# One kernel of six sublayers: two tensors for the scatter-adds of the first expert layer, and smaller edits at the ends of three stages

## Chip, core and metric

The kernel runs on one core of one Trainium2 chip. The metric is device time in microseconds from launch to end. Engines are named as in the profile: PE is TensorE, DVE VectorE, ACT ScalarE, POOL GpSimd, SP SyncE (here it only issues DMAs). One profiled execution gives every number of the trace.

## What is computed

Tokens are 8192 rows of 128 numbers. Six sublayers follow each other, each on the layer-normed (attention and routed feed-forward) or plain stream:

```python
x = x + 0.5 * _L0_ffn_ref(_layernorm(x), ...)    # f1: light local attention on all tokens, heavy attention on routed ones
x = x + _L0_attn_ref(_layernorm(x), ...)         # la: causal attention with latent q, k, v
x = x + 0.5 * _L0_ffn_ref(_layernorm(x), ...)    # f2
x = x + 0.5 * _L1_ffn_ref(_layernorm(x), ...)    # m1: top-6 of 64 experts, and a shared expert
x = x + _L1_attn_ref(_layernorm(x), ...)         # ca: attention with normalized q and k, no mask
x = x + 0.5 * _L1_ffn_ref(_layernorm(x), ...)    # m2: as m1
```

What matters of the expert layer and of the attention after it:

```python
def _L1_ffn_ref(x, ...):          # 64 experts, 6 of them per token
...
    hmid = gelu(einsum('ech,ehf->ecf', xs, w1))
    y = einsum('ecf,efh->ech', hmid, w2).reshape(E * CAP, h)
    y_pair = y[slot] * pair_w[:, None]
    out = zeros((t, h)).at[token_of].add(y_pair)
    shared = gelu(x @ sw1.T) @ sw2.T
    return out + shared
...
def _L1_attn_ref(x, ...):
    qkv = x @ in_proj_weight.T + in_proj_bias
    attn = softmax(l2_normalize(q) @ l2_normalize(k).T * ls)
```

In `_L0_attn_ref` q, k and v are `(x @ W_down) @ W_up`, half of each head's q and k turned by rope: pairs (x1, x2) become (-x2, x1) times a sine and added. In `_L0_ffn_ref` a routing score is the dot product of each normed token with two routing tokens.

## The kernel before

The stream stays on chip in `g_x` or `g_y` (128 partitions x 64 tiles of 128 numbers); `routed_ffn` (f1, f2), `stacked_attention` (la, ca) and `moe_block` (m1, m2) run one after another, and each begins when all engines have finished the one before. Within a stage every engine has its own instruction list, written out by hand as a function `body`, and the engines wait for each other by semaphores only.

**Expert layer, `moe_block`.** The base of the result (`m_ob`: stream and shared expert) is stored to the DRAM tensor `x_after_experts`. The picked tokens are worked on in 24 chunks of 128 rows, three to a group. POOL gathers a chunk (`gather`, line 2218: an indirect DMA from `gather_table` into `m_xs`); PE transposes it (line 2332) and multiplies by the experts' weights (2342, 2353, 2363, the last sums rows of equal token within a chunk); ACT copies a group's three results into `m_yc` (2422), one of two buffers. POOL then adds each chunk to `x_after_experts` by an indirect DMA with an add (line 2252). A token's rows can stand in several chunks, so a scatter-add waits until the one before it has landed (`scattered`), and only then goes out; after it POOL issues the gather of the chunk six further on. m2 does the same into `out_x`.

**Dense attention, `stacked_attention(latent=False)`.** It reads the stream back from `x_after_experts`: ACT's queue loads `g_y` in four parts of 16 tiles (1 MB each), SP's queue the weights, the biases, `ca_ones`, and rows of a block pattern. The attention is pipelined over 16 batches of 4 tiles; bodies -3, -2 and -1 fill the pipeline. `part_stats` (1872 to 1887) makes the layer norm's scale `g_a` and shift `g_b` of one part on DVE: 16 statistics (1876) and six small operations, with ACT's `deviation` (1751, 1753) in between. Part 0 comes ahead of body -3, parts 1, 2 and 3 at the ends of bodies -3, -2 and -1. In each body ACT makes the normed tiles `ca_xn` (1849), PE transposes them (1717), ACT copies them to `ca_xnT` (1858), PE multiplies (1580, 1666), ACT and DVE normalize (1924, 1839, 1841), POOL splits q and k into three bf16 parts (`split`, 1335 to 1347), SP stores those to `stack_image` (1299) and loads them back as `ca_qs`, `ca_ks` (1308). From body -1 on PE makes the scores (1484) and DVE their maxima (1936), 16 per body.

**Latent attention, its tail.** In every batch POOL multiplies the new stream with the routing tokens (`route_dots`, 1398) and sums the products by halving in seven steps (1408); the last batch's stand at the end of the stage.

**First light attention, its tail.** Here the weights `fw_weff` of the latent attention are made: products of `W_down` and `W_up` for q, k, v and two turned copies, whose `W_up` DVE has turned and negated before (`f1l_up`, 693 to 702, in front of the maximum of line 651). PE makes them in 5 x 8 fp32 products, which the profile shows as 80 instructions (553); ACT copies them (620, 621).

## Time and profile before

| | us |
|---|---|
| median of three runs | 3169.9 (3168.26 to 3171.17) |
| the profiled execution | 3158.49 |
| its span, first to last instruction | 3156.8 |

Where the stages lie in the span: f1 0 to 800 (its light attention ends at 542), la 800 to 1533, f2 1533 to about 2270, m1 from there to 2492 (its scatters 2388.6 to about 2487), ca 2492.8 to about 2930, m2 to the end. PE is busy for 86% of the span, DVE 73%, ACT and POOL 58% and 50%. In the profile an engine's idle time stands in brackets behind the instruction it ended at, with what ended it. "issue" means that nothing visible was waited for. A name ending in q (SPq, POOLq) is the engine's queue. Buffer numbers are left out.

### The profile page before, as it was taken

To read this page: it belongs to the slowest core of one execution; us is meant where nothing else is said; L and a number is where in the kernel's file an instruction comes from. 1 tells how busy PE (TensorE), PEld (TensorE's weight loads), DVE (VectorE), ACT (ScalarE), POOL (GpSimd) and SP (SyncE) were. 2 spreads that over 40 slices of the span, in tenths; PEclk is the share of its full clock that TensorE was granted. 3 is DMA by queue.
4 is the path that set the end of the run, shared out by engine and by line. 5 is a ranking of instruction groups with operands and counts; after the bars stand their busy time and mean duration, and the time that the engine had idled before them with its cause. 6 is when DMAs were issued, how large, how long until landed. Compare 5 with 4: busy or idle time off the path is not lost. (4 is left out here: it accounts for less than half of the span.)

```text
span 3156.8 us, 72883 instructions
## 1 busy us (share of the span) xinstructions
PE 2729.0 (86%) x24406; PEld 1826.4 (58%) x24406; DVE 2288.7 (73%) x6052; ACT 1825.7 (58%) x3760; POOL 1591.3 (50%) x1872
## 2 busy tenths in 40 slices
PE   7999998999599999999788999899895369998874
PEld 4777887777233333333477888677773135555652
DVE  5998775888489988887488777699782267775741
ACT  3777664555156666666477666455551148786521
POOL 1222323876447766664322232577555356662555
PEclk9999998999689999999899999899995569998875
DMA  4000000000233333331000000000063346553532
GB/s 112 1 0 1 1 0 1 1 0 1 74 82 82 82 82 77 76 75 41 14 0 0 1 1 0 1 1 0 18 158 69 81 124 151 143 140 92 145 91 30
DMA packets 155616, 161.59 MB, mean 51 GB/s; under 512 B 42001, under 2 KB 133905, under 8 KB 154641
## 3 DMA queue, kind: packets, MB, share of 16 engines
q1 hardware_dynamic: 145616, 146.90, 18.7%
q0 software_dynamic: 9216, 7.87, 1.9%
q10 hardware_dynamic: 576, 4.19, 0.3%
q8 instruction: 113, 1.85, 0.3%
q14 instruction: 95, 0.77, 0.1%
HBM read 83.24 MB, written 74.60 MB: 50 GB/s over the span
## 5 line engine op out<-in xcount | busy, mean ns | idle before, releaser
L1938 DVE CUSTOM_DVE_ANT_0 la_ps<-la_ps,la_tri 128x512 f32<-128x512 f32 (+3 forms) x1024 | 481.5, 514 | 93.6 <-PE la_ps L1484 86.6
L1762 ACT ACTIVATE la_prob<-la_ps 128x512 f32<-128x512 f32 x640 | 373.8, 602 | 240.2 <-PE la_ps L1495 233.2
L475 POOL TENSOR_TENSOR f2l_prob<-f2l_prob,f2l_rec 128x512 f32<-128x512 f32 x128 | 133.0, 1060 | 330.6 <-DVE f2l_rec L673 330.6
L475 POOL TENSOR_TENSOR f1l_prob<-f1l_prob,f1l_rec 128x512 f32<-128x512 f32 x128 | 133.0, 1060 | 328.5 <-DVE f1l_rec L673 328.5
L1484 PE MATMUL la_ps<-la_ks,la_qs 48*128 48x512 bf16 (+3 forms) x1024 | 255.0, 317 | 47.2 <-DVE la_mx L1938 29.2
L1350 POOL TENSOR_SCALAR_AFFINE_SELECT la_prob<-la_prob 128x512 f32<-128x512 f32 x256 | 159.3, 634 | 208.9 <-ACT la_prob L1762 208.6
L1495 PE MATMUL la_ps<-la_qs,la_ks 50*128 50x512 bf16 (+3 forms) x1024 | 241.4, 308 | 5.2 <-ACT la_prob L1762 2.2
L1936 DVE TENSOR_REDUCE ca_mx<-ca_ps 128x4 f32<-128x512 f32 x256 | 173.7, 687 | 90.9 <-PE ca_ps L1484 89.6
L1495 PEld LDWEIGHTS la_ps<-la_qs,la_ks 50*128 50x128 bf16 x1024 | 66.9, 94 | 234.7 <-ACT la_prob L1762 163.1
L1762 ACT ACTIVATE ca_prob<-ca_ps 128x512 f32<-128x512 f32 x256 | 152.1, 602 | 85.0 <-PE ca_ps L1495 85.0
L1527 PE MATMUL la_ps_o<-la_prob,la_v 128*32 128x512 f32 (+3 forms) x2048 | 196.0, 456 | 0.0
L1938 DVE DVE_READ_ACCUMULATOR2_ANT la_mx<- 128x1 f32 x1024 | 144.8, 141 | 0.0
L1484 PEld LDWEIGHTS la_ps<-la_ks,la_qs 48*128 48x128 bf16 x1024 | 67.1, 95 | 115.9 <-DVE la_mx L1938 92.6
L504 PE MATMUL f2l_ps_qk<-f2l_xrT,fw_wqkv 128*128 128x128 f32 x1024 | 133.0, 284 | 0.7 <-ACT f2l_xrT L609 0.7
L504 PE MATMUL f1l_ps_qk<-f1l_xrT,fw_wqkv 128*128 128x128 f32 x1024 | 133.0, 284 | 0.7 <-ACT f1l_xrT L609 0.7
L504 PEld LDWEIGHTS f2l_ps_qk<-f2l_xrT,fw_wqkv 128*128 128x128 f32 x1024 | 120.7, 194 | 11.7 <-issue 10.5
L504 PEld LDWEIGHTS f1l_ps_qk<-f1l_xrT,fw_wqkv 128*128 128x128 f32 x1024 | 120.7, 194 | 11.7 <-issue 10.5
L592 ACT ACTIVATE f2l_prob<-f2l_ssub 128x1024 f32<-128x1024 f32 x64 | 67.8, 1059 | 85.4 <-DVE f2l_ssub L655 82.7
L592 ACT ACTIVATE f1l_prob<-f1l_ssub 128x1024 f32<-128x1024 f32 x64 | 67.7, 1058 | 80.5 <-DVE f1l_ssub L655 80.5
L1484 PE MATMUL ca_ps<-ca_ks,ca_qs 56*128 56x128 bf16 x1024 | 99.0, 225 | 5.2 <-DVE ca_mx L1936 3.0
L1495 PE MATMUL ca_ps<-ca_qs,ca_ks 58*128 58x128 bf16 x1024 | 99.4, 224 | 4.4 <-ACT ca_prob L1762 3.4
L1495 PEld LDWEIGHTS ca_ps<-ca_qs,ca_ks 58*128 58x128 bf16 x1024 | 58.4, 96 | 71.0 <-ACT ca_prob L1762 36.8
(539 smaller groups left out, 7977.8 us busy)
## 6 DMA issues: line engine op xcount, KB each, us to landing
stack_image<-la_parts SPq DMA_DIRECT2D x192, 128.0 KB, 2.4
stack_image<-ca_parts SPq DMA_DIRECT2D x192, 128.0 KB, 2.4
la_qs<-stack_image SPq DMA_DIRECT2D x64, 192.0 KB, 3.6
la_ks<-stack_image SPq DMA_DIRECT2D x64, 192.0 KB, 4.4
ca_qs<-stack_image SPq DMA_DIRECT2D x64, 192.0 KB, 3.5
ca_ks<-stack_image SPq DMA_DIRECT2D x64, 192.0 KB, 4.5
gather_table<-fw_wqkv SPq DMA_DIRECT2D x16, 256.0 KB, 2.4
gather_table<-m_pr SPq DMA_DIRECT2D x32, 128.0 KB, 2.3
```

The lines of the kernel that those rows point to most:

```text
L475: nc.gpsimd.tensor_tensor(pr[:, g], pr[:, g], rc[:, g].rearrange("p (h o) -> p h o", o=1).broadcast_to([P, PAIRS, P]), ALU.mult).then_inc( ...
L504: last = nc.tensor.matmul(ps_qk[:, t, p], wqkv[:, t, p * P:(p + 1) * P], xrT[:], start=True, stop=True)
L592: nc.scalar.activation(prob[(u - 1) % 2][:], ssub[:], ACT.Exp, scale=SM).then_inc(p_sb, 1)
L1350: return nc.gpsimd.affine_select(view, view, pattern=[[0, 4], [1, P]], compare_op=ALU.is_ge, fill=0.0, base=0, channel_multiplier=-1)
L1484: last = nc.tensor.matmul(bank[:, col:col + width], qs[u][rows, h // 2, qblk * P:(qblk + 1) * P], ks[u][rows, h // 2, keys], start=True, s ...
L1495: last = nc.tensor.matmul(bank[:, col:col + width], ks[u][rows, h // 2, blk * P:(blk + 1) * P], qs[u][rows, h // 2, blk * P:blk * P + widt ...
L1527: last = nc.tensor.matmul(ps_o[32 * j:32 * j + 32, blk * P:T], v[u][:, blk, 4 * q + j, :], prob[q % 2][:, unit, col:col + width], start=bl ...
L1762: nc.scalar.activation(prob[q % 2][:, n], ps2[n % 2][:], ACT.Exp, scale=SM).then_inc(S["p_sb"], 1)
L1936: last = nc.vector.tensor_reduce(m, bank[:].rearrange("p (a b) -> p a b", a=TPB), X_AX, ALU.max)
L1938: last = nc.vector.tensor_tensor_reduce(bank[:, col:col + width], bank[:, col:col + width], tri[:, T - width:T], 1.0, -BIG, ALU.add, ALU.m ...
```

## The change

Four edits.

1. `moe_block` takes a second tensor. In m1 the even chunks are added into `x_after_experts`, the odd ones into the new `x_odd_chunks`; a scatter waits only for the one before the last. `reach` sets the gathers: two after each of the first three scatters, then one, of the chunk nine further on, until chunk 23. m2 has no second tensor and stays.
2. `x_odd_chunks` is cleared by five SP DMAs from a zeroed tile, at the start of f2's light attention.
3. The dense attention loads both tensors and adds them (`y += odd`). The parts now end at tiles 8, 24, 44 and 64. Part 0 comes on ACT's queue; part 1 on SP's behind the weights; parts 2 and 3 behind the block rows. DVE adds and makes statistics piecewise, between the other work of the bodies: part 1 in four pieces in body -3, parts 2 and 3 in 16 pieces in bodies -2 and -1. The arithmetic of part 1 is in body -3, of part 2 in body -1, of part 3 in body 0; ACT's `deviation` moves into the bodies.
4. The last route dots' halving on POOL is one DVE reduce. PE makes only the three straight weight products (48 instructions), ACT copies once, and DVE makes the turned copies from the result, in eight small operations.

```diff
@@ light_attention
...
-            up2 = A.sb("up2", [P, 5, 2, AD])
+            up2 = A.sb("up2", [P, 3, 2, AD])
...
+            if cleared is not None:
+                sp.wait_ge(zero_ready, 1)
+                rows = cleared.rearrange(RUNS, p=P)
+                for n in range(5):
+                    sp.dma_start(rows[:, 13 * n:13 * n + 13], zero[:].broadcast_to([P, 13, C])).then_inc(zero_stored, 16)
+                sp.wait_ge(zero_stored, 80)
...
-                    for n in range(5):
+                    for n in range(3):
...
-                    nc.scalar.copy(weff[:, 0:4], ps_s[:, 0])
-                    nc.scalar.copy(weff[:, 4], ps_s[:, 1, 0])
+                    nc.scalar.copy(weff[:, 0:3], ps_s[:, 0, 0:3]).then_inc(weff_sb, 1)
...
+                if at(i, NT + 2) and weff is not None:
+                    dve.wait_ge(weff_sb, 1)
+                    dve.wait_ge(turned_clear, 1)
+                    for t in range(2):
+                        straight, turned = (weff[:, k].rearrange("p (h d) -> p h d", h=AH) for k in (t, 3 + t))
+                        for d in range(4, AD, 2):
+                            nc.vector.tensor_scalar(turned[:, :, d:d + 1], straight[:, :, d + 1:d + 2], -1.0, None, ALU.mult)
+                            nc.vector.tensor_copy(turned[:, :, d + 1:d + 2], straight[:, :, d:d + 1])
@@ stacked_attention
...
-        PARTS = 4
-        NPART = NT // PARTS
+        BOUNDS = (0, 8, 24, 44, 64)
+        PARTS = len(BOUNDS) - 1
+        STATS_IN = {-3: 1, -2: 2, -1: 3}
+        MATH_IN = {-3: 1, -1: 2, 0: 3}
...
+        def load_part(eng, n):
+            for to, rows in zip((y, odd), source):
+                eng.dma_start(to[:, part(n)], rows.rearrange(RUNS, p=P)[:, part(n)]).then_inc(x_in[n], 16)
...
-                    for part in range(3):
-                        route_dots(B - 1, part)
+                    route_dots(B - 1, 0)
...
+            def part_tiles(n, tiles):
+                ts = slice(tiles[0], tiles[-1] + 1)
+                ch.step(nc.vector.tensor_tensor(y[:, ts], y[:, ts], odd[:, ts], ALU.add))
+                for j in tiles:
+                    last = nc.vector.bn_stats(stats[:, j], y[:, j])
...
+            def part_stats(n, k):
+                size = BOUNDS[n + 1] - BOUNDS[n]
+                over = 4 if n == 1 else 16
+                if k == 0:
+                    dve.wait_ge(x_in[n], 32)
+                    nc.vector.nop(nofuse=True)
+                if k < over:
+                    part_tiles(n, range(BOUNDS[n] + size * k // over, BOUNDS[n] + size * (k + 1) // over))
...
+                if i == B and q == 3 and n == UQ - 1:
+                    dve.wait_ge(S["dot_step"], 8 * (B - 1) + 1)
+                    nc.vector.tensor_reduce(dots[:, :, TPB * (B - 1):TPB * B], prod[:], X_AX, ALU.add)
...
+                if part_of(STATS_IN, i):
+                    part_stats(part_of(STATS_IN, i), k)
+                m = part_of(MATH_IN, i)
+                if m == 1 and k == 5:
+                    part_math(m, range(4))
+                if m and m > 1 and k in (2, 5, 7, 10):
+                    part_math(m, ((2, 5, 7, 10).index(k),))
+                if m and k == 14:
+                    part_math(m, (4,))
@@ moe_block
...
+        def reach(c):
+            if second is None:
+                return min(c + 6, NCH), min(c + 7, NCH)
+            return min(6 + 2 * c if c < 3 else c + 9, NCH), min(8 + 2 * c if c < 3 else c + 10, NCH)
...
-                if c:
-                    pool.wait_ge(S["scattered"], 16 * c)
-                nc.gpsimd.indirect_dma_start(out=xo[:, :], out_offset=bass.IndirectOffsetOnAxis(ap=sidx[:, c:c + 1], axis=0),
+                if c >= SR:
+                    pool.wait_ge(scattered[c % SR], 16 * (c // SR))
+                nc.gpsimd.indirect_dma_start(out=sums[c % SR][:, :], out_offset=bass.IndirectOffsetOnAxis(ap=sidx[:, c:c + 1], axis=0),
...
-                if c + 6 < NCH:
-                    gather(c + 6)
+                for ahead in range(*reach(c)):
+                    gather(ahead)
```

Three places show what moves. The first is POOL in m1, from the first scatter on; the lines 2252 and 2218 of before are 2317 and 2283 after. Before:

```order
797 L2252 DMA x_after_experts<-m_yc,m_sidx 8320x128
798 L2218 DMA m_xs<-gather_table,m_gidx 128x192
799 L2252 DMA x_after_experts<-m_yc,m_sidx 8320x128
800 L2218 DMA m_xs<-gather_table,m_gidx 128x192
801 L2252 DMA x_after_experts<-m_yc,m_sidx 8320x128
```

After:

```order
792 L2317 DMA x_after_experts<-m_yc,m_sidx 8320x128
793 L2283 DMA m_xs<-gather_table,m_gidx 128x192 x2
794 L2317 DMA x_odd_chunks<-m_yc,m_sidx 8320x128
795 L2283 DMA m_xs<-gather_table,m_gidx 128x192 x2
796 L2317 DMA x_after_experts<-m_yc,m_sidx 8320x128
797 L2283 DMA m_xs<-gather_table,m_gidx 128x192 x2
798 L2317 DMA x_odd_chunks<-m_yc,m_sidx 8320x128
799 L2283 DMA m_xs<-gather_table,m_gidx 128x192
```

Two gathers stand behind each of the first three scatters, and the scatters alternate between the tensors.

The second is DVE in the dense attention: the end of body -2 and the start of body -1, with the maxima (line 1936 before, 1982 after). Before, the sixteen statistics and six operations stand in one piece between `ca_t` and the next body's work, here those of part 2 ahead of the first maximum:

```order
3621 L1924 TENSOR_SCALAR ca_t_1<-ca_ps_c 128x512
3622 L1876 BN_STATS g_stats<-g_y 128x6 x16
3623 L1879 TENSOR_TENSOR ca_total<-g_stats 128x16
3624 L1880 TENSOR_TENSOR ca_var<-g_stats 128x16
3625 L1881 TENSOR_TENSOR ca_diff<-g_stats 128x16
3626 L1882 TENSOR_TENSOR ca_diff<-ca_diff 128x16
3627 L1883 SCALAR_TENSOR_TENSOR ca_var<-ca_diff,ca_var 128x16
3628 L1884 TENSOR_SCALAR ca_var<-ca_var 128x16
3629 L1886 SCALAR_TENSOR_TENSOR g_b<-ca_total,g_a 128x16
3630 L1936 TENSOR_REDUCE ca_mx<-ca_ps_0 128x4
```

After, an add and one or two statistics stand between any two other operations:

```order
3661 L1900 BN_STATS g_stats<-g_y 128x6 x2
3662 L1982 TENSOR_REDUCE ca_mx<-ca_ps_0 128x4
3663 L1898 TENSOR_TENSOR g_y<-g_y,ca_odd 128x128
3664 L1900 BN_STATS g_stats<-g_y 128x6
3665 L1982 TENSOR_REDUCE ca_mx<-ca_ps_1 128x4
3666 L1898 TENSOR_TENSOR g_y<-g_y,ca_odd 128x128
3667 L1900 BN_STATS g_stats<-g_y 128x6
```

What stood ahead of the first maximum is spread over two bodies.

The third is SP at the start of the dense attention. Before, the images (`stack_image`) follow the last of the block rows:

```order
225 L1211 DMA ca_qs<-in_block_q 8x8x512
226 L1213 DMA ca_ks<-in_block_k 10x8x512
227 L1211 DMA ca_qs<-in_block_q 8x8x512
228 L1213 DMA ca_ks<-in_block_k 10x8x512
229 L1299 DMA stack_image<-ca_parts 16x8x512 x12
```

After, two loads of part 1 (128x2048, line 1281) stand right behind `ca_ones`, ahead of the block rows, and four loads of parts 2 and 3 behind those:

```order
230 L1229 DMA ca_qs<-in_block_q 8x8x512
231 L1231 DMA ca_ks<-in_block_k 10x8x512
232 L1281 DMA g_y<-x_after_experts 128x2560
233 L1281 DMA ca_odd<-x_odd_chunks 128x2560
234 L1281 DMA g_y<-x_after_experts 128x2560
235 L1281 DMA ca_odd<-x_odd_chunks 128x2560
236 L1325 DMA stack_image<-ca_parts 16x8x512 x12
```

The loads of `y` have moved from ACT's queue, which keeps part 0 only.

## Rows read from the trace of the kernel before

**Rows 1.** page: clock granted to TensorE and DMA share, in 40 slices of 78.9 us

```profile
PEclk9999998999689999999899999899995569998875
DMA  4000000000233333331000000000063346553532
```

**Rows 2.** timeline of POOL, scatter stretch: start, us, work, [idle before <-releaser]

```profile
2388.57 1.62 POOL L2252 DMA_INDIRECT x_after_experts<-m_yc,m_sidx  x1 [8.18 <-ACT m_yc L2422]
...
2398.67 0.99 POOL L2218 DMA_INDIRECT m_xs<-gather_table,m_gidx  x1 [0.30 <-issue]
2400.97 1.58 POOL L2252 DMA_INDIRECT x_after_experts<-m_yc,m_sidx  x1 [1.31 <-DMA x_after_experts<-m_yc,m_sidx]
...
2464.01 1.59 POOL L2252 DMA_INDIRECT x_after_experts<-m_yc,m_sidx  x1 [1.40 <-DMA x_after_experts<-m_yc,m_sidx]
...
2484.39 1.55 POOL L2252 DMA_INDIRECT x_after_experts<-m_yc,m_sidx  x1 [2.47 <-DMA x_after_experts<-m_yc,m_sidx]
2492.84 3.54 POOL L1218 MEMSET ca_v<- 128x2048 f32 x2 [6.90 <-POOLq L51]
```

**Rows 3.** timelines of ACT and PE in the same stretch

```profile
2387.16 0.48 ACT L2422 COPY m_yc<-m_ps_o 128x384 f32<-128x384 f32 x1 [5.53 <-PE m_ps_o L2363]
...
2395.67 0.48 ACT L2422 COPY m_yc<-m_ps_o 128x384 f32<-128x384 f32 x1 [5.53 <-PE m_ps_o L2363]
...
2410.71 0.48 ACT L2422 COPY m_yc<-m_ps_o 128x384 f32<-128x384 f32 x1 [5.53 <-PE m_ps_o L2363]
...
2401.92 0.90 PE L2332 MATMUL m_ps_t<-g_ident,m_xs 128*128 128x128 f32 x3 [6.29 <-DMA m_xs<-gather_table,m_gidx]
```

**Rows 4.** timeline of DVE, start of the dense attention

```profile
2498.41 3.19 DVE L1876 BATCH_NORM_STATS2 g_stats<-g_y 128x6 f32<-128x128 f32 x16 [26.33 <-DMA g_y<-x_after_experts]
...
2509.74 0.29 DVE L1894 TENSOR_SCALAR ca_wc<-ca_wc,ca_hsc 128x128 f32<-128x128 f32 x1 [6.34 <-DMA ca_ones<-in_ones]
...
2522.35 3.18 DVE L1876 BATCH_NORM_STATS2 g_stats<-g_y 128x6 f32<-128x128 f32 x16
...
2525.66 1.14 DVE L1880 TENSOR_TENSOR ca_var<-g_stats 128x16 f32<-128x16 f32 x1
```

**Rows 5.** windows, start of the dense attention: busy (count) by engine, PEclk, DMA share, GB/s

```profile
2495.00:2500.00 5.00, 0.00 (x0) 0.00 (x0) 1.59 (x9) 1.28 (x1) 1.70 (x3) 0.50 1.01 412
```

**Rows 6.** timeline of ACT, ends of the first three bodies

```profile
2530.50 0.22 ACT L1751 ACTIVATE ca_diff<-ca_var 128x16 f32<-128x16 f32 x1 [6.65 <-DVE ca_var L1884]
...
2575.91 0.22 ACT L1751 ACTIVATE ca_diff<-ca_var 128x16 f32<-128x16 f32 x1 [9.70 <-DVE ca_var L1884]
```

**Rows 7.** operations of line 630 by form: shortest/median/longest ns

```profile
L630 DVE SCALAR_TENSOR_TENSOR f1l_xr<-g_x,g_a,g_b x30: 301/1170/1215, 53.9 to 263.9; 128x128 f32 x24, 128x128 f32<-128x128 f32 x6
```

**Rows 8.** timelines of POOL, SP and PE: split, image stores, first scores

```profile
2521.88 1.26 POOL L1335 TENSOR_TENSOR ca_rr<-ca_qb,ca_t 128x512 f32<-128x512 f32 x1 [25.12 <-ACT ca_t L1841]
...
2528.02 9.76 SPq L1299 DMA_DIRECT2D stack_image<-ca_parts  x12
...
2546.00 0.43 PE L1484 MATMUL ca_ps<-ca_ks,ca_qs 56*128 56x128 bf16 x8 [2.21 <-DMA ca_ks<-stack_image]
```

**Rows 9.** timeline of POOL, end of the latent attention

```profile
1528.24 3.92 POOL L1408 TENSOR_TENSOR la_prod<-la_prod 128x512 f32<-128x512 f32 x6
```

**Rows 10.** timeline of DVE, ends of both light attentions

```profile
505.72 1.21 DVE L669 TENSOR_REDUCE f1l_rsum<-f1l_prob 128x8 f32<-128x1024 f32 x1
...
509.89 1.22 DVE L651 TENSOR_REDUCE f1l_mx<-f1l_ps_s 128x8 f32<-128x1024 f32 x1
...
1996.90 1.23 DVE L651 TENSOR_REDUCE f2l_mx<-f2l_ps_s 128x8 f32<-128x1024 f32 x1 [1.29 <-PE f2l_ps_s L537]
```

**Rows 11.** end of the first light attention: timeline of PE, and a window

```profile
524.14 12.68 PE L553 MATMUL f1l_ps_s<-f1l_up,f1l_wdT 128*128 128x16 f32 x80
...
524.00:528.00 4.00, 4.00 (x39) 4.00 (x37) 1.46 (x5) 0.98 (x2) 0.00 (x0) 1.00 0.01 4
```

**Rows 12.** window of one full body of the dense attention

```profile
2600.20:2622.40 22.20, 20.65 (x307) 12.73 (x307) 15.86 (x35) 17.74 (x36) 14.39 (x16) 1.00 0.63 148
```

More of the change, by code:

```diff
@@ L467, in _ @@
             nc.gpsimd.memset(ones[:], 1.0).then_inc(filled, 1)
+            if cleared is not None:
+                nc.gpsimd.memset(zero[:], 0.0).then_inc(zero_ready, 1)
+            if weff is not None:
+                nc.gpsimd.memset(weff[:, 3:5], 0.0).then_inc(turned_clear, 1)
             def body(i, u, d, r):
@@ L1290, in _ @@
                 load_weights(sp)
+                for n in range(2, PARTS):
+                    load_part(sp, n)
             def store_parts(b, u, t):
@@ L1743, in _ @@
             if not latent:
-                for n in range(PARTS):
-                    act.dma_start(y[:, part(n)], source.rearrange(RUNS, p=P)[:, part(n)]).then_inc(x_in[n], 16)
+                load_part(act, 0)
                 nc.scalar.preload_act_table_set("natural_log_exp_and_others")
@@ L1843, in make_xn @@
             def make_xn(b, tiles=range(TPB)):
-                if not latent and isinstance(b, int) and b * TPB % NPART == 0 and tiles[0] == 0:
-                    act.wait_ge(S["shift_ready"], b * TPB // NPART + 1)
+                if not latent and isinstance(b, int) and b * TPB in BOUNDS and tiles[0] == 0:
+                    act.wait_ge(S["shift_ready"], BOUNDS.index(b * TPB) + 1)
                 if past(b, 1):
@@ L1870, in _, with part_math @@
             ch = Chain(dve, S["n_step"])
-            def part_stats(n):
+            def part_tiles(n, tiles):
[3 more added lines that the diff above has]
+                    last = nc.vector.bn_stats(stats[:, j], y[:, j])
+                if tiles[-1] == BOUNDS[n + 1] - 1:
+                    ch.step(last)
+            def part_math(n, steps):
                 p = part(n)
-                dve.wait_ge(x_in[n], 16)
-                for j in range(NPART * n, NPART * n + NPART):
-                    last = nc.vector.bn_stats(stats[:, j], y[:, j])
-                ch.step(last)
@@ L1891, in _ @@
             else:
-                part_stats(0)
+                dve.wait_ge(x_in[0], 32)
+                nc.vector.nop(nofuse=True)
+                part_tiles(0, range(BOUNDS[1]))
+                part_math(0, range(5))
                 dve.wait_ge(S["w_in"], W_IN)
@@ L2134, in moe_block @@
         gathered = [A.sem(f"gathered{u}") for u in range(GR)]
+        sums = [xo] if second is None else [xo, second]
+        def reach(c):
+            if second is None:
+                return min(c + 6, NCH), min(c + 7, NCH)
+            return min(6 + 2 * c if c < 3 else c + 9, NCH), min(8 + 2 * c if c < 3 else c + 10, NCH)
+        SR = len(sums)
+        scattered = [A.sem(f"scattered{u}") for u in range(SR)]
         uses = lambda n, ring, u: len(range(u, n, ring))
```

76 lines of the change are left out of this document (42 added, 34 removed).

## The prediction, made before the changed kernel was run

> **What bounds the kernel now.** I read the page first: on one core no engine is full for the whole span, and the TensorE clock dips to half in four places, one of them the end of the first expert layer and the start of the dense attention [rows 1]. So the question for each edit is which engine ends last in its own stage, and I went to the timelines.
>
> First expert layer, scatter stretch (2388.6 to about 2487). The reader is to see in POOL's timeline a strict cycle: scatter-add 1.58 us, gap 0.30, gather 0.99, then idle until the DMA of that same scatter has landed [rows 2]. From the first scatter to the nineteenth (2464.01) it takes (2464.01 - 2388.57)/18 = 4.19 us each; the last five steps, which have no gather, take (2484.39 - 2464.01)/5 = 4.08, of which 2.5 is idle. So the landing of one scatter, not POOL's own work, sets the pace. TensorE is not the limit: ACT's `m_yc` copies stand 8.5 us apart when data is there [rows 3], against 3 x 4.19 = 12.6 per group of three chunks.
>
> Start of the dense attention. DVE's first statistics wait for part 0 of `y`, but TensorE's first transposes wait for DVE's `ca_wc` at 2509.74, which waits for `ca_ones`, a small load that shares the DMA engines with 4 MB of `y` [rows 4, 5]. Then ACT waits for a lump of 16 statistics and their arithmetic at the end of each of the first three bodies: 6.65 us, about that once more, then 9.70 [rows 6].
>
> **The change part by part.** The sum is made against the profiled execution (3158.5 us; its span is 3156.8). It lies 11.4 us under the median of 3169.9, so a difference found on it is taken off the median unchanged.
>
> *Scatters into two tensors.* The first scatter stays where it is (2388.57, waits for ACT). A scatter with one gather now costs POOL 1.58 + 0.30 + 0.99 + 0.30 = 3.2 us, one with two gathers 4.5, and one without may start when the one before the last has landed: 4.08/2 = 2.04. There are three with two gathers, twelve with one, and eight steps after that: 2388.6 + 3 x 4.5 + 12 x 3.2 + 8 x 2.04 = 2456.8 for the last scatter, against 2484.4: -27.6. Is the compute ready? A gather's data is in use 3.25 us after its issue (2398.67 to 2401.92) and `m_yc` begins 8.8 after that [rows 2, 3]. Gather 8 goes out at about 2395, so `m_yc` of group 2 is there by 2407.5, and its scatter's turn comes at 2411. Later groups follow each 8.5, slower than nothing on POOL until the tail: group 7 is ready at 2450.5, its scatter's turn is 2453. That is close, so I take **-27**. The worse bound is -22: two scatters in flight land 1 us later each (0.5 x 8 = 4) and 0.3 us more per group. The better bound is -29, with POOL's shortest durations. Nothing else queued on POOL waits for the new waits.
>
> *Start of the dense attention, loads.* ACT's queue now carries 2 x 0.5 MB for part 0, the same megabyte as the old part 0, so it should land as before, at stage start + 5.6. DVE adds 128x1024 (other operations on 1024 elements take 1.21 [rows 10]; I book 1.4 for two inputs), 8 statistics at 0.2, arithmetic 1.6: +10.2. `ca_ones` no longer competes with 4 MB, and the rest of the loads stand behind it in SP's order. ACT's `ca_xn` follows and TensorE starts at +12.1, where before it could not start until `ca_wc` was done at +17.3: -5.2.
>
> *The lumps.* Body -3 without its lump of 6.65 ends near 2519 in the old clock of the trace (was 2530.5; -5.2 and -6.6). Part of it comes back, since DVE now does in bodies -2 and -1 what it did not do before, 32 small adds with 36 statistics. The row to price an add from is the two-input DVE operation on 128x128 in the first light attention, beside a working POOL: its median and its shortest are in [rows 7], 1.2 us and 0.30 us. In this very ramp a 128x16 operation on two SBUF inputs took 1.14 instead of 0.18 while POOL ran its `split`; the 16 statistics right before it took 3.18 in all, 0.2 each, as ever [rows 4]. POOL's `split` runs ten operations of 1.2 us per body [rows 8], so about half of the adds of a body meet one. For body -2 I take 16 x 1.45 = 23 us on DVE (add, statistic and half a lock), so that the maxima of body -1 begin at 2542.5 instead of 2551.2. They could not begin before 2541 at any price: the scores need the images, which leave POOL, are stored by SP in 9.76 us and come back 18 us after the first store [rows 8], and this chain moves by the 5.2 only. Body -1 is then DVE's: 16 x (0.65 + 0.3 + 0.25) + 3.3 for its copies and arithmetic + 5 of locks = 27.5, ending at 2570 against 2576.3 [rows 6]; body 0 gives about 1 back to the arithmetic of part 3. I take **-5**. Bounds: -12 with no lock at all (2541 + 23.5), +6 with every one of the 32 adds at 1.2. The extra 5 MB of parts 2 and 3 stand in SP's queue before the first image store. 8 MB at the 412 GB/s that the start reached [rows 5] is about 20 us; SP's first store comes 35 us after the start now and 30 then, so they are hidden with 5 to 8 us of room.
>
> The Trainium skill, "SBUF", section "Who interferes with whom", speaks against this part: a DVE instruction with two SBUF inputs and a GpSimd instruction that reads SBUF exclude each other for the whole of an instruction, whichever came first. The 1.14 us row agrees with it, and the sixteen statistics just before it, with one input, were not slowed. Taken to the letter for each add, the ramp would end at +6 and the total at 3138 instead of 3127.
>
> *Last route dots of the latent attention.* The six halvings on POOL, 3.92 us [rows 9], and the small seventh step go; one DVE reduce of 1024 elements, 1.21 us [rows 10], comes. Nothing stands beside them: the next stage waits. 3.92 + about 0.3 for the small last step - 1.21 = **-3.0** (bounds -2 and -3.2).
>
> *Effective weights at the end of the first light attention.* 80 TensorE instructions become 48. The row shows 12.68 us for the 80; the window 524 to 528 holds 39 of them in 4.0 us at the full granted clock [rows 11], after which the clock falls to half. 48 of them end by about 5.3, so up to 7.4 goes; by equal shares it is 12.68 x 32/80 = 5.1. Eight small DVE operations (0.17 each) are added behind the copy, beside work that ends the stage. I take **-7** (bounds -4.3 and -8.5; the latter if the last two matmul groups also keep the full clock).
>
> *`up2` on DVE.* Eight tiny operations go from just ahead of a maximum. That maximum begins with no idle at 509.89, where its twin in the second feed-forward idles 1.29 us for TensorE [rows 10]. So at most 1.3 to 1.6 goes: **-1.3** (bounds 0 and -1.6).
>
> *Clearing the second tensor, two memsets.* 4.3 MB are stored in the second light attention, in which the DMA row of the page is 0 for 480 us [rows 1], by SP, which has nothing else to do there: **0** (bounds 0 and +1).
>
> Sum: -27 - 5 - 3 - 7 - 1.3 = -43.3, so 3115.2 for the profiled execution and 3169.9 - 43.3 = **3127**.
>
> **The rivals.**
> *A: scatters don't overlap.* The queue handles one indirect transfer at a time, so a scatter (2.5 us after POOL has written it) and a gather (3.25 - 0.99 = 2.3) follow each other: 4.8 for each pair x 15 + 2.5 x 8 = 92 against 95.8, -4 instead of -27: 3150. Against it: the gather of 2398.67 was in use after 3.25 us although a scatter had been written right before it, and a scatter behind a gather lands after 2.6 us of waiting, one without after 2.5 [rows 2, 3].
> *B: the lock meets every add*, +6 instead of -5: 3138. For it stand the 24 operations with a median of 1.2 [rows 7]; against it that POOL has only ten operations per body.
> *C: everything falls well.* The ramp gains 12, TensorE's clock stays up at the end of the first light attention: -8.5: 3118.
> *D, the one that ends slower: a late clock.* TensorE runs at half clock through the scatter stretch and the ramp, and rises in body 0. A full body is 22.1 us with 20.65 us of TensorE at the granted clock 1.00 [rows 12]. If bodies -1 and 0, now bound by DVE, keep TensorE too idle for the rise, each body at half clock costs up to 41 - 22 = 19 more. One such body leaves 3146; it decides from three bodies on: 3127 + 57 = 3184. Against it: body 0 before was just as thin and got its clock.
>
> **How the numbers follow.** The forecast 0.62, A 0.06, B 0.13, C 0.10, D 0.04, and 0.05 for combinations (A with B is 3161). Worse bounds of all terms together give -22 + 6 - 2 - 4.3 + 0 + 1 = -21; but they don't fall together, and 3148 is reached at once by the forecast's bad end or by B with a smaller scatter gain. The better end is -29 - 12 - 3.2 - 8.5 - 1.6 = -54, at 3116. The range is 3114 to 3148. Faster by over 0.2% (6.3 us, about what a measurement of this kernel can tell from no change) 0.92, within it 0.04, slower 0.04.
>
> **What would show it.** Scatters right: POOL's scatters 3.2 us apart, then about 2; the last one 68 us after the first. Under A they stay over 4 apart. Ramp right: TensorE's first transposes 12 us after the stage's first memset, no idle of ACT of 6 us for `ca_var`, adds of both 0.3 and about 1.2 us. If all are near 1.2, it is B. Weights right: 48 instructions in under 6 us. The forecast is wrong if a wait on `x_in` of part 2 or 3 shows, or if SP's stores stand behind the loads.

## The result, and the profile after

| | us |
|---|---|
| median of the changed kernel, four runs | 3125.3 (3119.5 to 3134.9) |
| median of the kernel before, four runs | 3169.1 (3151.8 to 3171.2) |
| ratio | 0.9872, 95% interval 0.9851 to 0.9892 |
| profiled execution, and its span | 3129.7, 3127.7 (before 3158.5, 3156.8) |

The medians are 43.8 us apart, the two profiled executions only 28.8. The first experiment shows where the 15 us between these two figures lie. The page of the changed kernel shows the dips of the granted clock where the page of before has them; the one at the end of the first expert layer is shorter (8757 where it read 9556):

```profile
PEclk9999998999689999999899999999987579998875
DMA  4000000000233333322200000000054556653532
```

The timeline of POOL in the scatter stretch answers to [rows 2]:

```profile
2392.95 1.62 POOL L2317 DMA_INDIRECT x_after_experts<-m_yc,m_sidx  x1 [8.28 <-ACT m_yc L2489]
2394.88 1.00 POOL L2283 DMA_INDIRECT m_xs<-gather_table,m_gidx  x1 [0.30 <-issue]
2396.19 0.95 POOL L2283 DMA_INDIRECT m_xs<-gather_table,m_gidx  x1 [0.30 <-issue]
2397.45 1.62 POOL L2317 DMA_INDIRECT x_odd_chunks<-m_yc,m_sidx  x1 [0.30 <-issue]
...
2409.61 1.60 POOL L2317 DMA_INDIRECT x_after_experts<-m_yc,m_sidx  x1 [0.31 <-issue]
2411.52 0.99 POOL L2283 DMA_INDIRECT m_xs<-gather_table,m_gidx  x1 [0.30 <-issue]
2412.81 1.59 POOL L2317 DMA_INDIRECT x_odd_chunks<-m_yc,m_sidx  x1 [0.30 <-issue]
...
2459.59 1.55 POOL L2317 DMA_INDIRECT x_after_experts<-m_yc,m_sidx  x1 [0.45 <-issue]
2461.55 1.55 POOL L2317 DMA_INDIRECT x_odd_chunks<-m_yc,m_sidx  x1 [0.41 <-issue]
2469.99 3.54 POOL L1236 MEMSET ca_v<- 128x2048 f32 x2 [6.89 <-POOLq L51]
```

The idle that ended at a DMA has gone. A scatter with two gathers takes 4.5 us, one with a gather 3.25, with nothing between them but the 0.30 of issue. The last nine go out 2.0 apart, half of the 4.08 of before. They still wait for a landing, though the profile calls the idle "issue": POOL's own 1.55 and 0.30 make only 1.85. The last scatter starts 68.6 us after the first, where it was 95.8.

The start of the dense attention, DVE and PE, answers to [rows 4] and [rows 8] (its first memset is at 2469.99):

```profile
2475.90 1.23 DVE L1898 TENSOR_TENSOR g_y<-g_y,ca_odd 128x1024 f32<-128x1024 f32 x1 [21.35 <-DMA ca_odd<-x_odd_chunks]
...
2480.45 0.28 DVE L1940 TENSOR_SCALAR ca_wc<-ca_wc,ca_hsc 128x128 f32<-128x128 f32 x1
...
2482.36 1.08 PE L1742 MATMUL ca_ps_b<-g_ident,ca_xn 128*128 128x128 f32 x4 [26.11 <-ACT ca_xn L1873]
...
2518.31 0.62 PE L1509 MATMUL ca_ps<-ca_ks,ca_qs 56*128 56x128 bf16 x8 [5.12 <-DMA ca_ks<-stack_image]
```

Part 0 is added at once (1.23 us), `ca_wc` no longer waits for anything, and TensorE starts 12.4 us after the memset; before it was 17.3. The first scores come at 48.3 and wait for an image; before at 53.2.

In bodies -2 and -1 (DVE, then POOL):

```profile
2500.66 1.03 DVE L1898 TENSOR_TENSOR g_y<-g_y,ca_odd 128x128 f32<-128x128 f32 x1
...
2506.97 0.27 DVE L1898 TENSOR_TENSOR g_y<-g_y,ca_odd 128x128 f32<-128x128 f32 x1
...
2519.03 0.69 DVE L1982 TENSOR_REDUCE ca_mx<-ca_ps 128x4 f32<-128x512 f32 x1 [1.18 <-PE ca_ps L1509]
...
2500.23 1.32 POOL L1361 TENSOR_TENSOR ca_rr<-ca_qb,ca_t 128x512 f32<-128x512 f32 x1
```

The add of one tile takes 1.03 us while POOL runs its `split` and 0.27 when POOL has finished. The first maximum is at 49.0. Body 0 begins (ACT's `ca_xnT`) at 76.7 us instead of 83.9. The windows of the whole body, changed and then before, show the granted clock at 0.99 and at 0.78:

```profile
2546.66:2566.60 19.94, 16.98 (x254) 9.91 (x253) 15.38 (x33) 16.42 (x34) 13.20 (x16) 0.99 0.49 111
```

```profile
2576.74:2600.15 23.41, 20.44 (x253) 11.10 (x253) 13.62 (x26) 16.09 (x32) 10.49 (x13) 0.78 0.41 102
```

The ends of the first light attention and of the latent attention answer to [rows 9], [rows 10] and [rows 11]:

```profile
522.68 6.81 PE L567 MATMUL f1l_ps_s<-f1l_up,f1l_wdT 128*128 128x16 f32 x48
529.41 1.98 PE L576 MATMUL f1l_ps_v<-f1l_probT,f1l_v 128*64 128x128 f32 x16
...
507.72 1.23 DVE L664 TENSOR_REDUCE f1l_mx<-f1l_ps_s 128x8 f32<-128x1024 f32 x1 [0.84 <-PE f1l_ps_s L551]
...
514.44 1.23 DVE L664 TENSOR_REDUCE f1l_mx<-f1l_ps_s 128x8 f32<-128x1024 f32 x1 [1.18 <-PE f1l_ps_s L551]
```

```profile
1532.31 1.22 DVE L2040 TENSOR_REDUCE fw_dots<-la_prod 128x8 f32<-128x1024 f32 x1 [1.67 <-POOL la_prod L1424]
...
1534.58 0.26 POOL L280 MEMSET f2r_wide<- 128x192 f32 x1 [2.31 <-POOLq L51]
```

48 weight instructions took 6.81 us. The granted clock fell to half within them, and what follows ran at half clock (1.98 us for 16 matmuls). The DVE reduce takes 1.22 us, and the next stage begins 2.3 us after its start.

Where the time went, by marks in the two profiled executions (us, changed minus before):

| stretch | forecast | measured |
|---|---|---|
| start to the end of the first light attention | -8.3 | -6.7 |
| latent attention without its tail | 0 | +10.8 |
| its tail | -3 | -3.2 |
| second feed-forward (with the clearing) | 0 | +0.3 |
| first expert layer up to the first scatter | 0 | +3.1 |
| first to last scatter | -27 | -27.2 |
| dense attention | -5 | -7.1 |
| second expert layer | 0 | +0.9 |

The stretches that the change was expected to move did move. Without the +10.8 of the latent attention, whose code the change does not touch, the marks add up to -39.9 us.

### The profile page after: what moved, and what is told of

Read it like the earlier page. It is cut to its first block and busy times, and to the rows that moved or that the text cites. A ratio compares the mean times of both kernels' runs of the same rounds, so it can differ in the third digit from the quotient of the medians.

```text
span 3127.7 us, 72866 instructions
## 1 busy us (share of the span) xinstructions
PE 2741.0 (88%) x24374; PEld 1829.6 (58%) x24374; DVE 2304.0 (74%) x6090; ACT 1826.1 (58%) x3759; POOL 1589.8 (51%) x1867
## 3 DMA queue, kind: packets, MB, share of 16 engines
q8 instruction: 113, 1.85, 0.3%
## 5 line engine op out<-in xcount | busy, mean ns | idle before, releaser
L1552 PE MATMUL la_ps_o<-la_prob,la_v 128*32 128x512 f32 (+3 forms) x2048 | 202.4, 470 | 0.0
L518 PEld LDWEIGHTS f2l_ps_qk<-f2l_xrT,fw_wqkv 128*128 128x128 f32 x1024 | 120.7, 194 | 11.7 <-issue 10.5
L518 PEld LDWEIGHTS f1l_ps_qk<-f1l_xrT,fw_wqkv 128*128 128x128 f32 x1024 | 120.5, 193 | 11.7 <-issue 10.5
L1520 PEld LDWEIGHTS ca_ps<-ca_qs,ca_ks 58*128 58x128 bf16 x1024 | 58.3, 96 | 68.6 <-ACT ca_prob L1786 36.7
```

What stands on the lines that cost most here:

```text
L518: last = nc.tensor.matmul(ps_qk[:, t, p], wqkv[:, t, p * P:(p + 1) * P], xrT[:], start=True, stop=True)
L1520: last = nc.tensor.matmul(bank[:, col:col + width], ks[u][rows, h // 2, blk * P:(blk + 1) * P], qs[u][rows, h // 2, blk * P:blk * P + widt ...
L1552: last = nc.tensor.matmul(ps_o[32 * j:32 * j + 32, blk * P:T], v[u][:, blk, 4 * q + j, :], prob[q % 2][:, unit, col:col + width], start=bl ...
```

## Experiments

**The same kernel again, and the kernel before again.** No edit in either.

> The changed kernel once more, nothing altered. Theory: the parts that the change touches repeat to within 1 us (first to last scatter 68.6 us, from the first memset of the dense attention to the first `ca_xnT` copy of body 0 76.7 us), while the latent attention (from its first memset to the first memset of the next feed-forward, 741.2 us here, 733.6 in the kernel before) comes out anywhere between about 730 and 745, because the granted clock drops for short spells there at other places in each execution. Then the profiled difference of 29 us and the median difference of 44 differ by such spells alone. Rival: the change itself slows the latent attention by about 8 us, then it is again near 741.

> The kernel before once more, nothing altered, for a second profile of it. Open is why the stretch of the first expert layer ahead of its first scatter is 117.6 us in every profile of the changed kernel and its variants, and 114.5 in the one of the kernel before, with a drop of the granted clock to half at about 32 to 42 us into the stage in the former only. Theory (the drop comes and goes with where the stage stands in time, not with the code): this profile can show either, and the latent attention, 725.6 us without its tail in the first profile, moves by several us. Rival (the kernel before never has the drop): 114.5 again, latent attention 733.6 again.

The changed kernel's median was 3129.9 us this time, against 3167.7 (ratio 0.9865, 0.9841 to 0.9889). By marks (us; "body 0" is where it begins after the stage's first memset, and how long it takes):

| | latent attention without tail | first expert layer to first scatter | first to last scatter | body 0 begins, its length |
|---|---|---|---|---|
| before | 725.6 | 114.5 | 95.8 | 83.9, 23.4 |
| before again | 739.0 | 114.7 | 96.9 | 82.8, 23.4 |
| changed | 736.4 | 117.6 | 68.6 | 76.7, 19.9 |
| changed again | 742.3 | 117.7 | 68.0 | 77.4, 19.9 |

The latent attention moves by 13 us between two profiles of one and the same kernel. With the change it is not always long either: 726.2 us in the run below with the edit of the first expert layer undone. Windows of 40 us in the middle of it, before and changed (columns: busy us and count for PE, PE loads, DVE, ACT, POOL, then PEclk, DMA share, GB/s):

```profile
1280.00:1320.00 40.00, 38.44 (x302) 13.99 (x300) 34.91 (x144) 26.43 (x50) 27.54 (x38) 0.96 0.32 77
```

```profile
1280.00:1320.00 40.00, 38.41 (x272) 13.89 (x271) 32.02 (x128) 24.96 (x47) 26.87 (x38) 0.87 0.29 70
```

TensorE is busy all the time in both, but where the granted clock averages 0.87 it gets through 272 instructions and not 302. So a part of the kernel that keeps PE fully busy gains and loses about 10 us by spells of half clock, and the whole time of one profiled pair is no measure of a change of this size; the marks of the stages are a better one. Without the latent attention the second pair's marks add up to -45.7 us, the first pair's to -39.9; the medians' 43.8 lies between. The first theory stood. The second, that the 3.1 us ahead of the first scatter come and go too, fell: 114.7 again. The clock takes another course there, with the same instructions. In the kernel before (second profile), from the stage's start, 32 us and then 10 us:

```profile
2287.74:2319.74 32.00, 24.42 (x151) 23.24 (x152) 22.48 (x124) 25.48 (x58) 25.08 (x46) 0.70 0.47 126
2319.74:2329.74 10.00, 9.09 (x82) 7.03 (x81) 9.55 (x53) 6.29 (x13) 6.91 (x12) 1.00 0.77 188
```

and in the changed one:

```profile
2275.36:2307.36 32.00, 22.28 (x157) 20.66 (x157) 22.57 (x118) 25.66 (x59) 24.82 (x47) 0.81 0.46 126
2307.36:2317.36 10.00, 9.64 (x41) 8.24 (x41) 9.55 (x50) 5.45 (x11) 6.99 (x11) 0.54 0.77 187
```

In the changed kernel the clock rose earlier, but then dropped to half once more, over the start of the wide products of the shared expert: 41 instructions in ten microseconds instead of 82. The run with the edit of the first expert layer undone shows below that this is not the only way to lose the 3 us.

**Scatters one behind the other, in two tensors.**

```diff
                 if c >= SR:
                     pool.wait_ge(scattered[c % SR], 16 * (c // SR))
+                if c and SR > 1:
+                    pool.wait_ge(scattered[(c - 1) % SR], 16 * ((c + 1) // 2))
```

> Two tensors and the gathers of the changed kernel, but each scatter-add also waits for the one right before it. Theory (the landing of a scatter sets the pace; what is won is won by two in flight): first to last scatter 3 x 4.5 + 12 x 4.19 + 8 x 4.08 = 96 us instead of 68.6, the whole kernel 27 us slower than the changed one. Rival (the gathers nine ahead keep the compute fed and bring most of it): under 80 us.

96.6 us from first to last scatter; 3155.9 us, ratio to before 0.9964 (0.9946 to 0.9982). POOL's timeline has the old waits, across the two tensors, of 1.2 us behind a gather and 2.5 without:

```profile
2418.81 1.80 POOL L2319 DMA_INDIRECT x_after_experts<-m_yc,m_sidx  x1 [1.24 <-DMA x_odd_chunks<-m_yc,m_sidx]
...
2489.41 1.55 POOL L2319 DMA_INDIRECT x_odd_chunks<-m_yc,m_sidx  x1 [2.48 <-DMA x_after_experts<-m_yc,m_sidx]
```

So the 27 us were the wait for the landing of the scatter before, and the deeper gathers by themselves win nothing.

**Two tensors, gathers six ahead.**

```diff
         def reach(c):
-            if second is None:
-                return min(c + 6, NCH), min(c + 7, NCH)
-            return min(6 + 2 * c if c < 3 else c + 9, NCH), min(8 + 2 * c if c < 3 else c + 10, NCH)
+            return min(c + 6, NCH), min(c + 7, NCH)
```

> Two tensors in flight as in the changed kernel, but the gathers six ahead as before the change. Theory: the last gather of group g then goes out after scatter 3g-4, and its result is there 1.9 + 3.25 + 8.8 + 0.5 = 14.4 us after that scatter's start; two groups take 6.4 + 14.4 = 20.8 us, 3.5 per scatter instead of 3.2, and the last scatter is 76 us after the first: 7 us slower than the changed kernel. Rival (POOL's own work is the bound with either reach): 68 to 69 us, no difference.

79.4 us from first to last scatter, 3.4 more than the 76 of the theory; the whole kernel took 3134.6 us, ratio to before 0.9905 (0.9879 to 0.9931). Two groups take 22.0 us (2386.54 to 2408.53) and not 20.8, and at each second group POOL waits:

```profile
2402.51 1.59 POOL L2316 DMA_INDIRECT x_odd_chunks<-m_yc,m_sidx  x1 [0.31 <-issue]
2404.40 0.99 POOL L2282 DMA_INDIRECT m_xs<-gather_table,m_gidx  x1 [0.30 <-issue]
2408.53 1.59 POOL L2316 DMA_INDIRECT x_after_experts<-m_yc,m_sidx  x1 [3.15 <-DVE m_sidx L2561]
```

The profile names DVE's `m_sidx`, but DVE makes the one of this group a group earlier; the wait is for `m_yc`, which ACT could copy only after PE had finished at 2407.2 (`m_ps_o`, 1.65 us from 2405.50). So both halves of this edit are needed: two in flight for 16 us, and the deeper gathers for the other 11.

**The edit of the first expert layer undone,** one tensor and six ahead, the rest of the change kept.

```diff
-                moe_block(nc, "m1", ..., lw["wqkv"], mid2)
+                moe_block(nc, "m1", ..., lw["wqkv"])
```

> The changed kernel with the edit of the first expert layer undone: one tensor, each scatter-add behind the one before, gathers six ahead. The second tensor is still cleared, loaded and added (all zeros). First theory: first to last scatter 95.8 us, kernel 27 us slower than the changed one. Open is the 3.1 us that every variant of the changed kernel loses ahead of the first scatter (117.6 us against 114.5 and 114.7 in two profiles of the kernel before), with the same instructions there and another course of the granted clock. If the new code of this stage causes it: 114.5 here. If what stands ahead of the stage causes it (clearing, timing of the stages before): 117.6 again.

96.9 us from first to last scatter, and 3160.6 us as a whole, 0.9979 (0.9963 to 0.9995): the rest of the change is worth 0.2%, some 7 us, by the timed runs, and about 9 by the marks of its profile (-5.8 first light attention, -3.2 tail, -7.4 dense attention to the end of body 0, +3.2 ahead of the first scatter, +3.0 in the second feed-forward, +1.1 in the scatters). Body 0 began at 78.8 us and took 21.1.

Ahead of the first scatter it still takes 117.8 us, so the stage's new code is not the cause. But the clock's course is not the same as in the changed kernel: the drop at 33 us lasts 3.4 us and not 10, and over the whole stretch the granted clock is 0.88, against 0.87 in the kernel before. Here the time went at full clock. DVE took longer for the same operations (this run, then before, 57 us from 9 us into the stage), and TensorE waited 3.0 us for its `m_mask`, where it had waited 0.6:

```profile
L2512 DVE SCALAR_TENSOR_TENSOR m_score<-m_pick,m_score 128x256 f32<-128x256 f32 x16 | 10.5, 655 | 0.0
L2510 DVE TENSOR_SCALAR m_mask<-m_pick 128x256 bf16<-128x256 f32 x16 | 8.5, 528 | 0.6
```

```profile
L2445 DVE SCALAR_TENSOR_TENSOR m_score<-m_pick,m_score 128x256 f32<-128x256 f32 x16 | 7.8, 485 | 0.0
L2443 DVE TENSOR_SCALAR m_mask<-m_pick 128x256 bf16<-128x256 f32 x16 | 6.6, 412 | 0.6
```

In the changed kernel `m_score` took 10.5 us in this stretch too. So the granted clock alone does not explain the 3 us.

**Statistics in lumps.** The pieces of adds and statistics of each part, with its arithmetic, stand after the body on DVE, and `deviation` after the body on ACT:

```diff
-                if part_of(STATS_IN, i):
-                    part_stats(part_of(STATS_IN, i), k)
...
+                m = part_of(STATS_IN, i)
+                if m:
+                    for k in range(4 if m == 1 else 16):
+                        part_stats(m, k)
+                    part_math(m, range(5))
```

> The dense attention with the same loads, bounds and adds, but adds, statistics and arithmetic of parts 1, 2 and 3 in one piece after bodies -3, -2 and -1, as the kernel before had its statistics. Theory (the pieces fill time in which DVE waits): a lump of 7.6 us after body -3 and of about 11.5 after bodies -2 and -1, so that body 0 starts 12 to 17 us later than 76.7 us after the first memset. Rival (the pieces cost in the bodies what the lumps cost behind them, and the gain at the start came from the loads alone): 0 to 4 us later.

Body 0 began at 100.9 us, 24 later and not 12 to 17, and the kernel took 3146.2 us (0.9919, 0.9902 to 0.9937). A row of ACT's waits (us in total, times, longest), then DVE and POOL:

```profile
ACT ca_diff L1775 <- DVE ca_var L1917: 32.8, 3, 15.4
...
2520.66 1.22 DVE L1898 TENSOR_TENSOR g_y<-g_y,ca_odd 128x128 f32<-128x128 f32 x1
2521.91 0.29 DVE L1900 BATCH_NORM_STATS2 g_stats<-g_y 128x6 f32<-128x128 f32 x1
2522.13 0.99 DVE L1898 TENSOR_TENSOR g_y<-g_y,ca_odd 128x128 f32<-128x128 f32 x1
...
2520.46 1.28 POOL L1365 TENSOR_TENSOR ca_parts<-ca_qb,ca_t 128x512 bf16<-128x512 f32 x1
2521.81 1.16 POOL L1368 TENSOR_TENSOR ca_r<-ca_rr,ca_parts 128x512 f32<-128x512 f32 x1
```

ACT waited 32.8 us for three lumps. The lump of part 2 began while POOL was still splitting, and nine adds of it took 0.7 to 1.2 us each: the add at 2520.66 ends within 0.15 us of POOL's operation of 2520.46, the next one within 0.15 us of the operation of 2521.81. POOL in its turn gets slower: beside the adds of four tiles after body -3 its operations take 1.48 and 1.60 instead of 1.15. ACT waits for the lump, so that these locks are waited for too; how much of the surplus over the theory they are was not priced.

**No adds.** In `part_tiles` the add is left out, so the odd chunks' share of the result is missing.

```diff
-                ch.step(nc.vector.tensor_tensor(y[:, ts], y[:, ts], odd[:, ts], ALU.add))
```

> The changed kernel without the additions of the second tensor in the dense attention (both tensors are still loaded; the odd chunks' share is left out of the result). It prices the adds. In the changed kernel the adds of body -2 take about 10 us and those of body -1 about 7.7, of which some 6.6 and 1.6 are above the 0.28 (one tile) and 0.42 (two tiles) that an add takes with POOL idle. Theory (DVE is the engine that ends last from the landing of part 2 to body 0, locks included): body 0 starts 8 to 14 us earlier than 76.7 us after the first memset. Rival (the way of the images through SP and back sets body -1, so the adds of body -2 cost nothing): 5 to 7 us earlier.

Body 0 began at 72.3, 4.4 and 5.1 us earlier than in the two profiles of the changed kernel; the whole took 3119.0 us (0.9839, 0.9809 to 0.9869). TensorE starts 1.1 us earlier without the add of part 0, but that gain is lost again by the first score. The theory fell, the rival came near:

```profile
2518.84 0.61 PE L1509 MATMUL ca_ps<-ca_ks,ca_qs 56*128 56x128 bf16 x8 [8.68 <-DMA ca_ks<-stack_image]
...
2519.55 0.69 DVE L1981 TENSOR_REDUCE ca_mx<-ca_ps 128x4 f32<-128x512 f32 x1 [9.58 <-PE ca_ps L1509]
```

DVE was idle for 9.6 us ahead of the first maximum, and PE for 8.7 ahead of the first score, until the image was loaded, 48.8 us after the memset: no earlier than with the adds (48.3). The adds of body -2, locks and all, cost nothing. From the first maximum to body 0 it took 22.8 us and not 27.7: the price is in body -1, 4.9 us for 6.7 us of adds.

**Part 3 added by POOL.**

```diff
                     if live(i, -2):
                         split(i + 2, 1, 2, 5)
+                    if isinstance(i, int) and i == -1:
+                        pool.wait_ge(x_in[3], 32)
+                        nc.gpsimd.nop(nofuse=True)
+                        for piece in range(5):
+                            ts = slice(BOUNDS[3] + 4 * piece, BOUNDS[3] + 4 * piece + 4)
+                            nc.gpsimd.tensor_tensor(y[:, ts], y[:, ts], odd[:, ts], ALU.add).then_inc(S["padd"], 1)
...
+                if n == 3:
+                    if k >= 6:
+                        first = 2 * (k - 6)
+                        dve.wait_ge(S["padd"], (first + 1) // 4 + 1)
+                        nc.vector.nop(nofuse=True)
+                        for j in range(first, first + 2):
+                            last = nc.vector.bn_stats(stats[:, BOUNDS[3] + j], y[:, BOUNDS[3] + j])
+                        if k == 15:
+                            ch.step(last)
+                    return
```

> The changed kernel, but the additions of part 3 (20 tiles) are done by POOL in five operations of four tiles, between its second split of batch 1 and the first maxima of batch 0, where it idles for about 9 us; DVE keeps the statistics, two per slot from the seventh slot of body -1 on. Theory (DVE is the bound of body -1): DVE is rid of 5.1 us of adds and 1.6 us of locks there, so that body 0 starts 4 to 7 us earlier than 76.7 us after the first memset, the whole kernel 4 to 7 us faster than the changed one. Rival (body -1 waits for images and for TensorE at half clock anyway): 0 to 2 us.

> The kernel with part 3 added by POOL once more, for a second profile. Theory: body 0 starts 70.7 us after the first memset again (76.7 and 77.4 in the changed kernel), 6 us won; the whole dense attention, 419.8 us there against 433.9 and 431.0, comes back to about 426, since more than 6 us of that was the granted clock's short drops. Rival (the further 7 us belong to the edit): 420 again.

Body 0 began at 70.7 and at 70.8 us, 6 to 7 us earlier than in the changed kernel. The adds stand in the hole POOL had, and DVE goes from maximum to statistics:

```profile
2530.61 6.15 POOL L1447 TENSOR_TENSOR g_y<-g_y,ca_odd 128x512 f32<-128x512 f32 x5
...
2538.72 0.69 DVE L1998 TENSOR_REDUCE ca_mx<-ca_ps 128x4 f32<-128x512 f32 x1
2539.33 0.47 DVE L1938 BATCH_NORM_STATS2 g_stats<-g_y 128x6 f32<-128x128 f32 x2
```

The whole kernel took 3126.1 us (0.9871, 0.9842 to 0.9899) in the first, 3121.3 (0.9848, 0.9816 to 0.9879) in the second; the changed kernel had 0.9872 and 0.9865. So the gain up to body 0 is shown, but the timed runs do not show that the whole is faster. The dense attention as a whole took 419.8 and 427.1 us (433.9 and 431.0 in the changed kernel); the further 7 us of the first did not come again. Part of them is body 0 itself, one and the same code: 20.3 us with a granted clock of 1.00 in the first profile, 23.3 us with 0.79 in the second.

**All loads at once on ACT's queue.**

```diff
-                load_part(sp, 1)
...
-                for n in range(2, PARTS):
-                    load_part(sp, n)
...
-                load_part(act, 0)
+                for n in range(PARTS):
+                    load_part(act, n)
```

> The changed kernel, but all four parts of both tensors (8 MB) are issued at once on ACT's queue, as the four parts of 4 MB were before; SP's queue keeps the weights, `ca_ones` and the block rows. Theory (TensorE's start was held by `ca_ones` landing among the large loads): TensorE's first transposes start 17 to 25 us after the first memset instead of 12.4, and body 0 shifts by the same 5 to 12 us. Rival (`ca_ones` lands in time whatever else is in flight, the earlier start is due to the smaller part 0): 12 to 13 us.

TensorE started at 27.9 us and body 0 at 94.0, a loss of 15 and 17 us, more than the ranges expected; the whole kernel took 3141.6 us (0.9913, 0.9883 to 0.9943).

```profile
2479.64 1.23 DVE L1896 TENSOR_TENSOR g_y<-g_y,ca_odd 128x1024 f32<-128x1024 f32 x1 [21.60 <-DMA ca_odd<-x_odd_chunks]
...
2501.16 0.29 DVE L1938 TENSOR_SCALAR ca_wc<-ca_wc,ca_hsc 128x128 f32<-128x128 f32 x1 [16.89 <-DMA ca_ones<-in_ones]
...
2501.55 1.09 PE L1739 MATMUL ca_ps_b<-g_ident,ca_xn 128*128 128x128 f32 x4 [41.80 <-DVE ca_wc L1938]
```

DVE had part 0 in time (2479.64, 5.9 us after the memset) and then stood for 16.9 us for `ca_ones`, 64 KB. It landed 27.4 us after the memset with 8 MB in flight, 0.3 us after the last of the large loads; with the 4 MB of the kernel before it landed at 16.9. The 4 MB more cost 10.6 us, some 395 GB/s, near the 412 of [rows 5]. So the early start is due to the order of the loads, not to the small part 0.

**Effective weights undone.** Five products, 80 instructions, `f1l_up` with its turned copies.

```diff
-                    for n in range(3):
+                    for n in range(5):
...
```

> The changed kernel with the edit of the effective weights undone (five products per pair in 80 TensorE instructions, `f1l_up` with its turned copies, two copies on ACT). Theory: the first heavy attention's first gate, at 536.5 us in the changed kernel and 543.2 in the kernel before, is back at 543; TensorE's weight group takes 12.7 us instead of 6.8, and the rest of the difference is `up2` on DVE. The same open question: ahead of the first scatter 117.6 us, or 114.5 if the shift of the start of everything by 6.6 us matters.

The first heavy attention's gate stands at 544.4 (536.5 in the changed kernel):

```profile
524.75 13.23 PE L565 MATMUL f1l_ps_s<-f1l_up,f1l_wdT 128*128 128x16 f32 x80
```

13.2 us for 80 against 6.8 for 48; 6.4 of the 7.9 us are this group. It was timed once, at 3134.7 us, which is too little to tell 7 us by. Ahead of the first scatter it was 116.3 us, neither of the two values.

## Why the prediction was right, and where it was not

The forecast was 3127, the median 3125.3. The step that carried it, the scatters, held in each of its parts: 4.5, 3.25 and 2.02 us per step, 68.6 us in all against a forecast of 68.2; -27.2 for -27. Rival A (no overlap) was wrong: the last scatters go out at half the old distance. The argument against A, from one gather behind one scatter, was right.

The loads: TensorE at 12.4 for 12.1, a gain of 4.9 for 5.2, and the run with all loads at once shows that the reason was right too.

The bodies: the forecast had the first maximum at 49.7 us from the memset (measured 49.0) and body 0 at 77 (measured 76.7), but one step on the way was wrong. It made body -2 a matter of DVE, 16 slots of 1.45 us, with half of the adds locked. The adds were locked much as priced (0.56 to 1.12 us for six of the first seven, 10 of the 16 in all), yet they cost nothing: the images set the first score, as the forecast's own bound of 2541 said, and without any add it comes no sooner. In body -1 three of the 16 adds took over 0.5 us.

The lock rule of the Trainium skill, "SBUF", section "Who interferes with whom", agrees with the rows on single instructions: an add of 0.27 us took 1.03 beside POOL's `split`. Rival B falls all the same. Its condition, a lock on every add, did not hold, and most of the locks that there were stood in body -2 under the wait for the images. Its +6 can't be had from the figures beside it either: the locks not yet booked, 8 more of 0.9 us in body -2 and 14.4 us in place of 5 in body -1, come to about +11.

The term for the dense attention as a whole was too small: -5 against -7.2 at body 0's start, -10.7 at its end, and -7.1 over the whole stage (-8.4 in the second pair of profiles). The step that failed is "body 0 gives about 1 back". It took 19.9 us instead of 23.4, since the granted clock rose 0.5 us after its start and not 10 us into it. Much speaks for luck here. With the same code in this stage body 0 took 23.2, 23.1 and 23.1 us in the runs with serial scatters, with gathers six ahead and with the weights undone, 19.9 twice in the changed kernel, and 20.3 and 23.3 in the two profiles of the kernel with POOL's adds. What decides it stays open. Rival D saw that the clock matters in body 0, but expected it to rise later than before, not sooner.

The weights: 48 instructions took 6.8 us, not 5.3. The step took the rate of the window at full clock for all 48, but the clock fell within them. In the second profile of the changed kernel it fell behind them, and the forecast's size came out:

```profile
523.04 5.43 PE L567 MATMUL f1l_ps_s<-f1l_up,f1l_wdT 128*128 128x16 f32 x48
```

So the term of -7 was -5.9 in the first profile and about -7.3 in the second. `up2` gave -0.4 for -1.3: the maximum came 1.4 us sooner, but the next one waited 1.18 us for PE, so that most of it was given back. The eight small DVE operations, which the forecast put at nothing as "beside work that ends the stage", stand behind the last other work of DVE there and cost 0.7 us: from its last `g_y` to the next stage's first copy it is 1.96 us, before 1.29. (In the first profile another 0.7 us was there at the stage's first window already; another run with the same code there began that window 0.3 us later than the kernel before, so this comes and goes.) The reduce, -3.2 for -3.0, and the hidden clearing (+0.3 for that feed-forward) were as priced.

What no step had: 3 us lost ahead of the first scatter, 116.3 to 120.2 us in all eleven profiles that have the change or most of it, 114.5 and 114.7 with the kernel before. Against it stand the 2.1 and 3.4 us by which the dense attention as a whole gained more than forecast, part of it by the clock in body 0. So the closeness of the total is in part luck.

Open: why the stretch ahead of the first scatter is longer. It isn't the new code of that stage, and half clock alone does not explain it, since the run with that code undone lost the 3 us at the clock of before. Moving the stage in time by the weights' 7 us changed it only by half. Leaving out the clearing of the second tensor wasn't tried.

## What to carry to other kernels

Where one engine waits for its own DMA to land before it may issue the next, a second target with the sum taken later can double the rate (4.1 to 2.0 us here where nothing stood between), but only if the supply is fetched further ahead too: here 16 us came from the one and 11 more from both. Put additional work into holes of an engine by asking what that hole waits for. What stood under another wait was free here, locks and all; what stood in the last body before the steady state was paid for. Compare changes of 1% by marks between stages of several profiles, since spells of half clock in untouched code moved one stage by 13 us between two profiles of one kernel.

## What the runs showed of the hardware

Two indirect DMAs with an add, to two tensors, are both in flight: scatters went out 2.0 us apart, and the twelve into `x_odd_chunks` landed 3.2 to 3.4 us after their start (the profile has no landings for the other tensor). One at a time they had landed after 3.2 to 3.7. With a gather between them it was 3.3 to 3.4, without 3.2 to 3.3.

The lock between POOL and DVE works both ways: DVE's two-input add of one tile took up to 1.26 us instead of 0.27, and POOL's operation of 1.15 us took 1.60 beside adds of four tiles.

A load of 64 KB, issued on another queue 4.4 us after the first of 8 MB of loads, took 23.1 us and landed with the last of them; behind 1 MB it took 3.2 us.

The same instructions of the latent attention took 725.6 and 739.0 us in two executions of the same kernel. The granted clock averaged 0.91 over that stage in the one and 0.89 in the other.
